# Moving the transposed maxima to another PSUM bank in a fused attention and normalization kernel

## The reference

```python
local = _local_attention(heads(q), heads(k), heads(v))   # 16 heads of 16 channels, window of 128 keys
...
rq = (x @ rq_w + rq_b)...                                # 4 latent heads over 64 pooled chunks
lattn = jax.nn.softmax(lscores, axis=-1)
remote = lat_out @ rout_w + rout_b
gate = jax.nn.sigmoid(local @ gl_w + remote_h @ gr_w)
mixed = gate * local + (1.0 - gate) * remote_h
return mixed @ out_w + out_b
```

## Time and profile before

| | |
|---|---|
| median of 3 runs | 580.47 us (572.05 to 580.49) |
| the profiled execution's own time | 576.64 us |
| its span, first to last instruction | 574.9 us |
| mean granted TensorE clock | 0.949 |
| busy share of the span | TensorE 84%, VectorE 76%, GpSimd 66%, ScalarE 62% |

### The profile page before, as it was taken

One profiled execution on the slowest core, in us unless ns is written; L12 is line 12 of the kernel. 1 busy time (PEld: TensorE's weight loads), 2 busy tenths in 40 slices (PEclk: granted clock), 3 DMA queues, 4 the chain that ended last, 5 costly groups with the idle time before them and its releaser, 6 DMA issues.

```text
span 574.9 us, 19855 instructions
## 1 busy us (share of the span) xinstructions
PE 482.9 (84%) x7168; PEld 364.1 (63%) x7168; DVE 436.6 (76%) x1193; ACT 353.8 (62%) x868; POOL 379.2 (66%) x516
## 2 busy tenths in 40 slices
PE   2446689999899999999999999999999999988771
PEld 2205567777677666777777676777776676766451
DVE  2155657788688888988988788888888887878554
ACT  1210466677677667777777577777776776766540
POOL 2222346778577767788877587777777677766663
PEclk9975889999899999999999899999999999999776
DMA  9558644618244444434252607162534444440000
GB/s 277 114 133 246 163 105 99 132 47 187 56 113 75 95 94 93 94 90 93 64 101 68 119 34 145 39 125 62 120 68 97 92 94 93 82 79 10 11 10 19
DMA packets 56523, 55.15 MB, mean 96 GB/s; under 512 B 7380, under 2 KB 53100, under 8 KB 54892
## 3 DMA queue, kind: packets, MB, share of 16 engines
q1 hardware_dynamic: 53564, 52.57, 41.4%
q10 hardware_dynamic: 2864, 1.31, 1.1%
HBM read 37.07 MB, written 16.80 MB: 94 GB/s over the span
## 4 chain that ended last, share of the span: by engine, by line
PE 72%; issue 11%; POOL 5%; DVE 4%; DMA 2%; ACT 2%; ACTq 1%; SPq 1%; POOLq 0%; DVEq 0%
PE p_pv L819 9%; PE p_qkv L730 9%; PE p_qkv L740 6%; PE p_misc L886 6%; PE p_y L806 5%; PE p_x L785 5%; PE p_y L807 5%; PE p_x L778 4%; PE p_a L751 3%; PE p_qkv L860 3%; PE p_misc L869 2%; PE p_a L831 2%; PE p_a L716 2%; PE p_misc L877 2%; PE p_a L753 2%
## 5 line engine op out<-in xcount | busy, mean ns | idle before, releaser
L592 ACT ACTIVATE pr<-p_y 128x512 f32<-128x512 f32 x224 | 124.6, 595 | 55.8 <-PE p_y L807 52.9
L1159 DVE TENSOR_REDUCE mtok<-p_x 128x3 bf16<-128x480 f32 (+1 forms) x192 | 109.3, 585 | 30.9 <-PE p_x L785 29.6
L441 POOL TENSOR_SCALAR_AFFINE_SELECT pr<-pr 128x512 f32<-128x512 f32 x128 | 89.6, 701 | 11.2 <-ACT pr L594 9.0
L451 POOL TENSOR_TENSOR rstd<-ve,half 128x1 f32<-128x1 f32 x96 | 58.1, 605 | 47.9 <-DVE ve L1079 47.7
L469 POOL TENSOR_TENSOR dif<-local,rem 128x272 f32<-128x272 f32 x32 | 30.9, 965 | 83.8 <-DVE local L1197 83.8
L445 POOL TENSOR_SCALAR_AFFINE_SELECT pr<-pr 128x512 f32<-128x512 f32 x112 | 81.3, 726 | 0.0
L807 PE MATMUL p_y<-qst,kst 112*128 112x128 bf16 x512 | 73.2, 221 | 0.0
L806 PE MATMUL p_y<-qst,kst 112*128 112x128 bf16 x448 | 66.5, 221 | 7.7 <-ACT pr L592 4.8
L819 PE MATMUL p_pv<-pr,vp 128*18 128x128 f32 x1920 | 67.1, 279 | 2.1 <-POOL pr L445 0.8
L730 PE MATMUL p_qkv<-hT,wqk 128*128 128x256 f32 x256 | 66.1, 403 | 2.2 <-DVE qkf L1111 1.3
L740 PE MATMUL p_qkv<-wv,hT 128*128 128x272 f32 x128 | 40.1, 439 | 29.5 <-issue 29.4
(11 more groups left out here) (131 smaller groups left out, 1092.7 us busy)
## 6 DMA issues: line engine op xcount, KB each, us to landing
scr_q<-terms SPq DMA_DIRECT2D x16, 384.0 KB, 2.5
qst<-scr_q SPq DMA_DIRECT2D x16, 384.0 KB, 4.7
scr_k<-terms SPq DMA_DIRECT2D x16, 384.0 KB, 4.4
kst<-scr_k SPq DMA_DIRECT2D x16, 384.0 KB, 5.4
qst<-scr_q SPq DMA_DIRECT2D x16, 256.0 KB, 5.4
kst<-scr_k SPq DMA_DIRECT2D x16, 256.0 KB, 6.4
out_y<-y SPq DMA_DIRECT2D x32, 128.0 KB, 1.7
x_all<-in_x SPq DMA_DIRECT2D x3, 1024.0 KB, 8.3
```

Source lines behind the costliest of these rows:

```text
L441: ins = pool.affine_select(out=own, in_=own, compare_op=ALU.is_ge, fill=0.0, base=-1, pattern=[[0, 4], [1, P]], channel_multiplier=-1)
L592: act.activation(pr[:, 2 * i:2 * i + 2, :, :], src, ACT.Exp).then_inc(exp_done[i], 1)
L1159: dve.tensor_reduce(mtok[:, KS + h0:KS + h1], p_x[i % 2][:, 0:(h1 - h0) * w].rearrange("p (h n) -> p h n", n=w), AX_X, ALU.max, negate=Tru ...
```

## The change

The transposed maxima are written to the first 64 columns of `p_pv`, where the value products of the tile before have just been copied out, instead of `p_qkv`. `max_t` now waits for that copy (`oT_ready`) in place of the projections' copies, and stands behind `scores(t,1)` in TensorE's slot. `project_v` and `lat_remote` no longer wait for the shift. On ScalarE the copy `out_t` becomes the first work of the slot, and `part2` comes after the shift.

```diff
--- before.py
+++ after.py
@@ -580,7 +580,7 @@
 
                 act.wait_ge(mT_psum, done(t))
                 act.wait_ge(st_psum[LAST_ST], done(t - 4))
-                act.activation(q_of(t)[KS:KS + H, :, :], p_qkv[KS:KS + H, 0:P // 2].bitcast(BF16).unsqueeze(1).to_broadcast([H, H, P]),
+                act.activation(q_of(t)[KS:KS + H, :, :], p_pv[KS:KS + H, 0:P // 2].bitcast(BF16).unsqueeze(1).to_broadcast([H, H, P]),
                                ACT.Copy).then_inc(shift_ready, 1)
 
             def exps(t, i):
@@ -640,14 +640,15 @@
             def slot(t, stages):
                 a, r, m, c = t + LEAD, t + 2, t - 1, t - 2
                 A, Q, S, T, C = ("A" in stages, "Q" in stages, "S" in stages, "T" in stages, "C" in stages)
-                if Q:
-                    part1(r)
                 if C:
                     out_t(c)
                 if Q:
+                    part1(r)
+                if T:
+                    shift(m)
+                if Q:
                     part2(r)
                 if T:
-                    shift(m)
                     lat_oT(m)
                 if S:
                     lat_exp(t)
@@ -734,7 +735,7 @@
             def project_v(t):
                 pe.wait_ge(hT_ready, done(t))
 
-                pe.wait_ge(shift_ready, done(t - 2))
+                pe.wait_ge(rem_ready, done(t - 3))
                 pe.wait_ge(qk_copied, done(t + 1))
                 for k in range(KC):
                     ins = pe.matmul(p_qkv[:, 0:H * (HD + 1)], hT[:, t % 4, k, :],
@@ -790,9 +791,8 @@
             def max_t(t):
                 pe.wait_ge(s_max[LAST_MAX], done(t))
 
-                pe.wait_ge(qk_copied, done(t + 3))
-                pe.wait_ge(rem_ready, done(t - 1))
-                pe.transpose(p_qkv[:, 0:P // 2].bitcast(BF16), mtok[:, :], ident_bf[:, :]).then_inc(mT_psum, 1)
+                pe.wait_ge(oT_ready, done(t - 1))
+                pe.transpose(p_pv[:, 0:P // 2].bitcast(BF16), mtok[:, :], ident_bf[:, :]).then_inc(mT_psum, 1)
 
             def scores_t(t, i):
 
@@ -856,7 +856,6 @@
                 pe.wait_ge(loT_ready, done(t))
 
                 pe.wait_ge(v_copied, done(t + 2))
-                pe.wait_ge(shift_ready, done(t))
                 pe.matmul(p_qkv[:, 0:D + H], loT[:, :], wro[:, :, :].rearrange("p h k -> p (h k)"), start=True, stop=True).then_inc(rem_psum, 1)
 
             def out_tokens(t):
@@ -891,10 +890,11 @@
             def slot(t, stages):
                 a, h, k, m, c = t + LEAD, t + 3, t + 1, t - 1, t - 2
                 A, PR, K, S, T, C = ("A" in stages, "P" in stages, "K" in stages, "S" in stages, "T" in stages, "C" in stages)
+                if S:
+                    scores(t, 1)
                 if T:
                     max_t(m)
                 if S:
-                    scores(t, 1)
                     scores(t, 0)
                     lat_scores(t)
                 if T:
```

## The result

| | before | after |
|---|---|---|
| median | 578.85 us (4 runs, 572.05 to 580.49) | 591.55 us (4 runs, 589.69 to 594.79) |
| profiled execution: its own time, span | 576.64, 574.9 us | 590.44, 588.7 us |
| mean granted TensorE clock | 0.949 | 0.936 |
| busy share | TensorE 84%, VectorE 76%, GpSimd 66%, ScalarE 62% | 84%, 75%, 63%, 59% |

The change makes the kernel slower: the ratio is 1.0248, with an interval of 1.0149 to 1.0348. The ratios in this text are taken from the fast runs alone, so they can differ from the quotient of two medians. The time lies close to the forecast of 589 us. How it is made up does not, as the rest of this text shows.

What follows compares the result with a forecast made beforehand. The start of GpSimd's `difference` was taken to set the slot (5.98 + 7.67 + 1.73 = 15.38 us). Terms 6.7 + 1.8 + 0.5 = +9.0 us, +1.6%, gave 589 us on the median of 580.47; range 576 to 604.

Steps and rivals of the forecast that it cites:

- 24 x 0.28 = +6.7 us: GpSimd's queue behind the late `part2`: `difference` starts at 6.26 instead of 5.98, lengthening 24 slots by 0.28 us each.
- the 7.67 and the 1.73 us: Slot's end: 7.67 us of gapless GpSimd work from `difference` to the last mask, then 1.73 to the next `out_t`; both stay.
- Nothing after `difference` shrinks: Rest of the slot after `difference`: the 7.67 us and 1.73 us stay, so +0.28 us a slot isn't taken back.
- the short slots did not absorb the 0.28: Three first-of-batch slots with half the masks: GpSimd waits for ScalarE's exponentials there, so the 0.28 us is absorbed.
- The +0.5 for the last slots: Last slots, without `part1`: the shift starts up to 0.4 us later, +0.5 us in all.
- start after VectorE's `scale2` instead of beside it: GpSimd's `difference` would shed its excess (757 ns least, 998 median), putting the sum near the lower end, -6 us over 24 slots.
- 2 x 0.9 = +1.8 us: Key load after two of the short slots, already late there: nothing covers its further delay, +1.8 us.
- if `scores(t,1)` waits for a DMA in every second slot: A sign, in the profile after, that the prediction is wrong: TensorE's scores waiting for a DMA load every second slot.
- +9.0 us: Sum of 6.7 + 1.8 + 0.5 on the profiled execution's 576.64 us, giving 585.6 us, or +1.6%.
- The key stack as the wait: Rival, chance 0.18: store still takes 4.4 us, load lands 2.5 us later, stalls of 14 + 5 us; +26 us, 607 us.
- the bubble is worth its length: Rival, chance 0.07: closing TensorE's idle time ahead of `project_v` shortens slots by up to 0.8 us; 19 us, 561 us.
- It cancels: Rival, chance 0.15: lower end of GpSimd's durations holds and key loads hide; no change, 580 to 584 us.

Runs made afterwards that it cites:

- ScalarE's order alone: The kernel before with only ScalarE's new order (`out_t`, `part1`, shift, `part2`), the maxima still in the projections' bank: 585.78 us, ratio 1.0119.
- `part1` first: The kernel after with `part1` ahead of `out_t` again, `part2` still behind the shift: 590.21 us, ratio 1.0228.
- the old ScalarE order: The kernel after with `part1` ahead of `out_t` and `part2` ahead of the shift again, new bank and TensorE order kept: 574.19 us, ratio 0.9954.
- the kernel before with the query load first: The kernel before with the query load put ahead of the output store on the sync engine's queue: 571.82 us, ratio 0.9944.
- the transpose ahead of the scores: The kernel after with `max_t` ahead of `scores(t,1)` again on TensorE: 587.68 us, ratio 1.0182.
- only with the query load first: The kernel after with ScalarE's old order and the query load ahead of the output store: 563.06 us, ratio 0.9762.
- with the query load first on both sides: The kernel after with ScalarE's old order and query load ahead of the output store, against the kernel before with that load order: 563.06 / 571.82, or 0.982.
- the kernel after with the query load first: The kernel after with the query load put ahead of the output store on the sync engine's queue: 586.71 us, ratio 1.0186.

## Why the prediction came out as it did

**Right: the mechanism on ScalarE and GpSimd.** The transpose at 0.74 (said: 0.70), the shift still at 1.13, `part2` at 3.03, `part3` at 3.74 (3.73), `difference` at 6.24 (6.26), no gap from `part3` to the last mask, no wait for `local` in ordinary slots, no idle time ahead of `project_v`. ScalarE's order alone and `part1` first show that `part2`'s place does it, and the old order that the bank alone wouldn't have.

**Mis-sized: "24 x 0.28 = +6.7 us".** The start of `difference` did move by 0.26, but the slot only by 0.08 on average, because the 7.67 and the 1.73 us did not stay. Behind `difference` the stretch to the last mask's end took 7.60 (`difference` itself 0.94 against 1.00). And from the mask's end to `out_t` it took 1.63. Before, TensorE came late to the last mask: its weight load for `sum_v` began at 359.03, 0.15 after the mask's end (358.25 + 0.63 = 358.88); after, it began at 383.82, 0.05 behind the end at 383.77. The last mask and that weight load, in the kernel before and in the one with ScalarE's order alone:

```profile
358.25 0.63 POOL L445 TENSOR_SCALAR_AFFINE_SELECT pr<-pr 128x512 f32<-128x512 f32 x1
359.03 1.23 PEld L819 LDWEIGHTS p_pv<-pr,vp 128*18 128x18 f32 x48 [0.33 <-POOL pr L445]
```
```profile
380.33 0.63 POOL L445 TENSOR_SCALAR_AFFINE_SELECT pr<-pr 128x512 f32<-128x512 f32 x1
381.01 1.01 PEld L820 LDWEIGHTS p_pv<-pr,vp 128*18 128x18 f32 x40 [0.42 <-POOL pr L445]
```

The second pair has the bubble still in it, and yet the same 0.05 and the same 1.63. So it isn't the freed TensorE time that pays the 0.10: TensorE had been late by that much, and the masks, which now come later in the slot, no longer wait for it. "Nothing after `difference` shrinks" is the step that failed. By the other side, the short slots did not absorb the 0.28: 7 and 23 grew by 0.3. Together the slots outside the stalls gave about +2.5 us instead of 6.7. The +0.5 for the last slots can't be read from the time: the shift starts 0.37 later in slots 29 and 30, as said, but these changed by -1.55 and +0.63 for reasons that weren't found.

The prediction had `difference` start after VectorE's `scale2` (L1225) instead of beside it. It doesn't. In the slots shown, `scale2`, before and after:

```profile
366.51 0.46 DVE L1225 SCALAR_TENSOR_TENSOR h2a<-x,mv,c 128x256 f32<-128x256 f32 x1
```
```profile
375.58 0.90 DVE L1225 SCALAR_TENSOR_TENSOR h2a<-x,mv,c 128x256 f32<-128x256 f32 x1
```

After, `scale2` runs beside `add_bias` (375.48 to 376.20), takes 0.90 us instead of 0.46, and still overlaps the first 0.31 us of `difference` (from 376.17), which takes 0.94 instead of 1.00. By the Trainium skill ("SBUF — State Buffer", Who interferes with whom) a VectorE instruction with two SBUF inputs contends with a GpSimd instruction that reads SBUF. The rows agree in that one of the two is long wherever they overlap; what `difference` takes beside no such instruction, the slots shown can't tell.

**Mis-sized: the key stack, "2 x 0.9 = +1.8 us".** The prediction had the place right (the slots behind short ones) and the store near right (2.5 us where its queue was empty), but the six late slots cost 13.5 us. Four things were missed. There are three slots behind short ones, not two: 8, 16 and 24; before, 16 was spared because slot 15 was 15.31 long, and after it is 14.15. That was chance of the one profile: in slot 15 `project_v` took 2.05 us instead of 1.16, at a granted clock of 0.53, and in the kernel before with the query load first the slot has 13.84. Slot 0, before which `part2` also stands behind a shift, wasn't counted, +4.5. In slots 7, 21 and 27 the store took 4.0 to 4.4 us although the query load was all but through (it lands 5.8 to 6.1 us after `out_t`, the store, issued at 4.93, at 8.9 to 9.4), which made slots 8, 22 and 28 late. And a late key stack now costs its whole length, since the transpose and the shift stand behind it: in slots 16 and 24 the shift was late by 1.35 and 1.01 us, and the slots longer than their neighbours 17 and 9 (15.34) by 1.34 and 0.98. The prediction named that link for the rival only; the transpose ahead of the scores shows its price. By the prediction's own list it is wrong "if `scores(t,1)` waits for a DMA in every second slot": TensorE does wait for keys in ordinary even slots too (0.28 us in slot 18, 0.35 in slot 20), but there the wait costs nothing, as the transpose still starts at 0.74 and the slot is 15.47 to 15.48 us long.

So the sum, +9.0 us, came near the measured 13.8 by luck: one term was 4 us too high and the other 12 us too low; the remainder is the slots outside both (-1.4), the earlier first `out_t` (-0.8) and the +0.5 that can't be seen.

**The rivals.** The key stack as the wait was right as a mechanism in six slots, not as it was put: the store didn't keep its 4.4 us in ordinary slots, and these don't stall. Nor is the late slots' 13.5 us what it gave (14 + 5 us, in other slots). That the bubble is worth its length was not so: with the old ScalarE order a slot in the middle of a batch gets 0.31 us shorter and others 0.74, where the rival had up to 0.8 in each, and only with the query load first does it show in the time. It cancels: no, though in ordinary slots it nearly did.

The Trainium skill ("Perfetto Trace Analysis", Optimization Strategy) tells to find the gaps on the engine that one optimizes for, and to make what blocks there start sooner or end faster. The runs agree, with a condition: the gap was 1.05 us a slot, closing it gave +2.5% with ScalarE's new order, -0.5% with the old one, and -1.8% with the query load first on both sides.

**What stays open.** Why single stores took 4.0 to 4.4 us with the query load through, and in the kernel after with the query load first as well (4.13 and 4.47 in slots 19 and 21), was not settled by a run. The records of the DMA packets point at something: of the 225 stores of terms in slots 2 and 4 to 27 of the nine kernels in which the query load is through, or within about a microsecond of it, when the key store is issued, 22 took more than 3.5 us. In each of these, 0.7 to 2.4 us after the store was issued, a packet of 16 KB started on the queue that the profile's page lists as instruction (q8), and took 0.9 to 1.6 us. Of the other 203 only one had such a packet start between 0.7 and 2.0 us; it took 3.47 us. So that packet is the likely cause, but no run moved it. The bank and TensorE's order were never tried apart with ScalarE's old order. Slots 10 and 12, +0.39 and +0.79, aren't explained by the landing of keys.

## What to carry to other kernels

When an instruction is moved on an in-order engine, follow its result past the next engine's queue to the DMA that it feeds: here a copy of 0.6 us, moved 2.5 us later, cost 0.1 us in an ordinary slot and 13.5 us in six slots in which the transfer behind it came late. Cure a late transfer first at its place in its own queue, then close the bubble: the same bank move was worth -0.5% before that and -1.8% after it. And don't put work that can go on behind work that waits for memory: the transpose behind the scores made a lateness of up to 1.5 us count, of which all but 0.2 us was hidden without it.

## What the runs showed of the hardware

**A stall can cost more than its length.** Five stretches of the kernel after around the first scores of slot 8, at 214.38: busy time and clock (from:to, us, then busy time with count for TensorE's matmuls and weight loads, VectorE, ScalarE and GpSimd, the granted clock, DMA share, GB/s):

```profile
205.70:211.70 6.00, 5.37 (x66) 3.56 (x63) 5.55 (x18) 1.90 (x7) 2.79 (x5) 1.00 0.70 104
211.70:214.40 2.70, 0.02 (x4) 0.05 (x5) 0.80 (x4) 1.08 (x2) 1.53 (x2) 1.00 0.75 112
214.40:215.90 1.50, 1.50 (x37) 1.15 (x37) 0.68 (x2) 0.84 (x1) 0.13 (x1) 1.00 0.04 11
215.90:219.30 3.40, 3.40 (x29) 2.46 (x28) 2.17 (x5) 3.19 (x12) 1.64 (x2) 0.56 0.00 0
219.30:221.20 1.90, 1.90 (x27) 1.31 (x25) 1.26 (x7) 1.28 (x3) 1.16 (x3) 0.89 0.56 207
```

After 2.78 us of idle TensorE the clock is still full at first, then near its lower level, 1.2 GHz, for some 3.4 us, with TensorE busy throughout, and `project_v` takes 2.18 us instead of 1.18. The shift's lateness alone (3.39 - 1.14 = 2.25) would put `difference` at 6.24 + 2.25 = 8.49; it came at 9.26. The other 0.77 goes with the lower clock: `difference` waited for `local` there, 0.74 us by the trace, and the work ahead of `local` for TensorE (L868). After the stall of slot 22 (1.84 us idle) it is alike, 0.55 over 3.5 us. Slots 16 and 24, with 1.89 and 1.54 us of idle time, show no such loss: there the lateness of the shift is all (6.24 + 1.35 = 7.59, as measured in slot 16). Nor does the length of the gap alone tell: in the kernel before, the bubble of 1.26 us ahead of `project_v`'s matmuls was followed by a granted clock of 0.53 over 2.2 us in slot 15, and by 1.00 in slot 17. What makes the difference wasn't tried.

**A store behind loads on the same queue.** The same 384 KB took 2.5 to 3.5 us from issue to landing where the loads ahead of it had landed or were within a microsecond or so of that (but for the single stores named above), and 4.4 to 4.8 at the median where these had 3 to 4 us to go. The longest, 7.7 us before and 7.4 with ScalarE's old order, stood in slot 3 behind a load of 1024 KB as well.
